# Layer 0's values into rows: three TensorE turnings of fp32, or one transposing DMA of two fp16 halves, in a two-layer graph transformer kernel on one core

## The chip, the core and the metric

The kernel runs on one core of one Trainium2 chip. The metric is the device time of one execution in microseconds, the median of several runs. The core has five engines that each follow an instruction stream of their own: TensorE (PE; its weight loads are shown apart as PEld), VectorE (DVE), ScalarE (ACT), GpSimd (POOL) and SyncE (SP), which here issues all the DMAs. The streams meet only at semaphores.

## What is computed

128 graphs of 128 nodes with 384 features go through two pre-norm attention layers of 12 heads (32 wide). The first masks its scores by the adjacency, the second takes the adjacency as a bias and has an output projection:

```python
h = relu(layernorm(x))                      # layer 0
q, k, v = h@Wq+bq, h@Wk+bk, h@Wv+bv         # 12 heads of 32
s = q@k.T/sqrt(32) + beta*adj;  s = where(adj > 0, s, -9e15)
x = x + softmax(s)@v                        # heads side by side
h = relu(layernorm(x))                      # layer 1
q, k, v = h@Wq.T, h@Wk.T, h@Wv.T+bv
x = x + (softmax(q@k.T*384**-0.5 + adj)@v)@Wo.T + bo
```

Everything is fp32 in and out. Where TensorE multiplies in fp16, a value is carried as two fp16 halves, high and low = value - high.

## The kernel before

**Units and phases.** Four graphs make a group and a group in one layer is a unit (`Unit`), 64 units in all. After the first few, units of layer 0 and layer 1 take turns. The kernel is a software pipeline over phases (`Phase`): in one phase one unit is normalised, the next older one is projected to q, k and v, the next is attended to, and the tail of the one before is finished. `run_phases` runs the first seven phases, then a loop of 12 pairs of phases a round, then the last ones. A phase has 12 slots (`SLOTS`), one for each chunk of four heads of a graph, so three slots a graph.

**The order is written out by hand.** Each engine's stream walks the slots and, within a slot, a few numbered places. A constant such as `O_T_AT = (3, 0)` says how many slots after the last chunk of a graph an operation stands, and at which place; `finished` turns that into slot and graph. Graph b's last chunk is slot 3b+2, so a constant (3, 0) puts the work of graphs 0, 1, 2 in slots 5, 8, 11 and that of graph 3 in slot 2 of the next phase, its tail. `NORM_SLOTS` does the same for the four norms of a phase (`normed_in`). `PROJ` spreads the 90 projection matmuls of a unit (ten jobs of nine, `project`, L999) over the slots: three counts a slot, for TensorE's places 0, 2 and 3. `HIGH_AT` and `LOW_AT` say where ScalarE and VectorE take a finished job's high and low half. No engine picks work; each takes its next instruction and waits if its semaphore is not there.

**Attention, per chunk.** TensorE makes scores (`scores`, L1012) two slots ahead, VectorE adds the bias and takes the maximum (`biased_scores`, L787) one slot ahead, ScalarE takes four exponentials with their sums (L667), TensorE turns the four fp32 probability tiles (`turn_probs`, L1022), and ScalarE copies them out of PSUM (`copy_turned`, L692). In layer 1 GpSimd also sums scores (L599, L605). After a graph's third chunk TensorE multiplies the turned probabilities with the values (`weigh_values`, L1035, into `o_bank`). The result lies feature by node, so it is the transpose of what the residual needs.

**Layer 0's way back to rows**, the part in question, once for each of 128 graphs:

- VectorE copies the 128x384 values of `o_bank` to `o_t` in SBUF, fp32 (`take_o`, L886), at (3, 0).
- TensorE turns the three 128x128 fp32 tiles of `o_t` into `post_bank` (`turn_rows`, L1050), at (3, 4).
- VectorE multiplies `post_bank` with the inverse softmax sums `inv0` into `o_rows` (`make_rows`, L908), at (4, 0).
- GpSimd adds the residual: `x_mid = x_res + o_rows` (`add_rows`, L618), at (4, 1). The layer-1 norm of the same group reads `x_mid`, in slots 0, 2, 3 and 5 of the phase in which graph 3's tail runs.

Layer 1 uses the same `post_bank` for its output projection (`project_out`, L1068 to L1072), after `norm_o` (L893), `high_o` on ScalarE (L706) and the low half on GpSimd (L644).

**The norm's own transposing DMA.** `split` (GpSimd, L585 to L590) leaves a graph's normalised rows as two fp16 halves in `h_rows`, [128, 2, 384], and SP brings them into `h` with one `dma_start_transpose` of six 128x128 tiles (L518), four for a unit. The q and k halves go to stacked buffers by plain DMAs, three for each of six jobs (`stack`, L483 and L487). All of these and the loads and stores (L496, L501, L509, L529, L539) stand in SP's one stream in a fixed order, and a wait there holds up what is behind it.

## Time and profile before

| | |
|---|---|
| median of 3 runs | 2221.32 us (2221.24 to 2221.51) |
| the profiled execution | 2218.76 us |
| its span, first to last instruction | 2216.9 us |
| busy share of the span | PE 97%, ACT 92%, DVE 82%, POOL 68% |
| mean granted TensorE clock | 0.998 |
| DMA | 303.38 MB, the queue's packets 71.2% of 16 engines' span |

Busy time is the union of an engine's instructions; issuing, waiting and branching do not count. A matmul's duration in the profile contains its way through the array, which the next matmul overlaps: what a matmul takes from the engine is the distance to the next one's start. Waits are inferred from semaphores. The profile is of one execution, 2.56 us under the median of the runs, and it leaves 1.9 us of its own time outside the span.

### The profile page before, as it was taken

To read this page: it belongs to the slowest core of one execution; us is meant where nothing else is said; L and a number is where in the kernel's file an instruction comes from. 1 tells how busy PE (TensorE), PEld (TensorE's weight loads), DVE (VectorE), ACT (ScalarE), POOL (GpSimd) and SP (SyncE) were. 2 spreads that over 40 slices of the span, in tenths; PEclk is the share of its full clock that TensorE was granted. 3 is DMA by queue.
4 is the path that set the end of the run, shared out by engine and by line. 5 is a ranking of instruction groups with operands and counts; after the bars stand their busy time and mean duration, and the time that the engine had idled before them with its cause. 6 is when DMAs were issued, how large, how long until landed. Compare 5 with 4: busy or idle time off the path is not lost.

```text
span 2216.9 us, 75650 instructions
## 1 busy us (share of the span) xinstructions
PE 2158.5 (97%) x19968; PEld 1422.1 (64%) x19968; DVE 1821.3 (82%) x10202; ACT 2049.2 (92%) x7824; POOL 1511.6 (68%) x2407
## 2 busy tenths in 40 slices
PE   5999999999999999999999999999999999999997
PEld 2566666666666666666666666666666666666665
DVE  5888888888888888888888888888888888888787
ACT  4999999999999999999999999999999999999987
POOL 1567766767667767667676677676676766776665
PEclk9999999999999999999999999999999999999999
DMA  9886776678678778675795686787767866766752
GB/s 191 168 134 140 130 138 147 130 131 157 126 137 138 137 143 141 132 143 125 134 159 127 136 139 136 145 136 137 143 130 135 154 130 134 146 132 134 133 103 60
DMA packets 461362, 303.38 MB, mean 137 GB/s; under 512 B 228481, under 2 KB 460929, under 8 KB 460929
## 3 DMA queue, kind: packets, MB, share of 16 engines
q1 hardware_dynamic: 460928, 298.45, 71.2%
q8 instruction: 169, 2.77, 0.6%
q14 instruction: 265, 2.16, 0.4%
HBM read 71.83 MB, written 25.17 MB: 44 GB/s over the span
## 4 chain that ended last, share of the span: by engine, by line
PE 84%; DVE 7%; ACT 4%; issue 3%; DMA 1%; SPq 0%; DVEq 0%; POOL 0%; ACTq 0%
PE job_bank L999 46%; PE pt_bank L1022 13%; PE o_bank L1035 8%; PE score_bank L1012 7%; ACT probs L667 3%; PE inv_bank L1058 3%; PE post_bank L1068 2%; PE post_bank L1069 2%; PE post_bank L1072 2%; PE post_bank L1050 2%; DVE neg L787 2%; DVE part_lo L865 1%; DVE inv_wide L857 1%; DMA x_norm<-in_x 1%; DVE off_zero L848 1%
## 5 line engine op out<-in xcount | busy, mean ns | idle before, releaser
L667 ACT ACTIVATE probs<-neg,neg_max 128x128 f32<-128x128 f32 x3072 | 1189.8, 394 | 47.0 <-DVE neg_max L787 47.0
L999 PE MATMUL job_bank<-h,w_hi 128*128 128x512 f16 x2304 | 725.9, 381 | 27.1 <-DMA h<-o_norm 21.6
L667 ACT ACTIVATION_READ_ACCUMULATOR probs<-neg,neg_max 128x1 f32 x3072 | 596.0, 194 | 0.0
L692 ACT ACTIVATE probs_t<-pt_bank 128x512 f32<-128x512 f32 x768 | 450.1, 586 | 32.0 <-PE pt_bank L1022 29.2
L1022 PE MATMUL pt_bank<-ident,probs 128*128 128x128 f32 x3072 | 464.2, 274 | 11.8 <-ACT probs_t L692 11.4
L999 PE MATMUL job_bank<-h,w_lo 128*128 128x512 f16 x1152 | 438.4, 381 | 0.0
L1022 PEld LDWEIGHTS pt_bank<-ident,probs 128*128 128x128 f32 x3072 | 365.9, 141 | 95.9 <-issue 14.0
L599 POOL TENSOR_TENSOR pair_sum<-neg 128x256 f32<-128x256 f32 x384 | 281.0, 732 | 196.0 <-DVE neg_max L787 180.8
L999 PE MATMUL job_bank<-w_hi,h 128*128 128x384 f16 x1536 | 413.9, 326 | 0.6 <-DVE v L879 0.3
L787 DVE CUSTOM_DVE_ANT_0 neg<-score_bank,bias 128x128 f32<-128x128 f32 x1536 | 354.1, 286 | 23.7 <-issue 22.2
L787 DVE CUSTOM_DVE_ANT_0 neg<-score_bank,adj 128x128 f32<-128x128 f32 x1536 | 353.8, 286 | 13.2 <-issue 10.5
L999 PEld LDWEIGHTS job_bank<-h,w_hi 128*128 128x128 f16 x2304 | 222.0, 98 | 217.4 <-issue 35.8
L1012 PEld LDWEIGHTS score_bank<-stack 96*128 96x128 f16 x3072 | 232.4, 97 | 126.5 <-DVE neg_max L787 6.3
L1012 PE MATMUL score_bank<-stack 96*128 96x128 f16 x3072 | 299.2, 219 | 5.3 <-DMA stack<-part_lo 5.3
L787 DVE DVE_READ_ACCUMULATOR2_ANT neg_max<- 128x1 f32 x3072 | 254.3, 83 | 0.6
L999 PE MATMUL job_bank<-w_lo,h 128*128 128x384 f16 x768 | 250.5, 326 | 0.0
L568 POOL TENSOR_TENSOR rstd<-shift_var,minus_half 128x1 f32<-128x1 f32 x256 | 144.8, 566 | 146.9 <-DVE shift_var L825 145.4
L590 POOL TENSOR_TENSOR h_rows<-h_rows 128x384 f16<-128x384 f32 x248 | 226.7, 914 | 20.7
L618 POOL TENSOR_TENSOR x_mid<-x_res,o_rows 128x384 f32<-128x384 f32 x128 | 127.9, 999 | 140.8 <-DVE o_rows L908 97.1
L1035 PE MATMUL o_bank<-probs_t,v 128*32 128x128 f32 x6144 | 220.8, 277 | 0.0
L870 DVE SCALAR_TENSOR_TENSOR part_lo<-job_bank,part_hi 128x512 f16<-128x512 f32 x192 | 132.5, 690 | 105.4 <-ACT part_hi L683 103.4
L605 POOL TENSOR_TENSOR four_sum<-pair_sum 128x128 f32<-128x128 f32 x384 | 176.6, 460 | 32.1
(75 smaller groups left out, 3507.6 us busy)
## 6 DMA issues: line engine op xcount, KB each, us to landing
stack<-part_hi SPq DMA_DIRECT2D x768, 128.0 KB, 3.5
stack<-part_lo SPq DMA_DIRECT2D x384, 128.0 KB, 3.8
x_res<-in_x SPq DMA_DIRECT2D x32, 768.0 KB, 5.8
out_x<-result_rows SPq DMA_DIRECT2D x128, 192.0 KB, 3.4
x_norm<-in_x SPq DMA_DIRECT2D x30, 768.0 KB, 6.2
adj<-in_adj SPq DMA_DIRECT2D x64, 256.0 KB, 3.8
h<-h_rows SPq DMA_TRANSPOSE x252, 3.9
x_norm<-in_x SPq DMA_DIRECT2D x4, 192.0 KB, 4.0
```

The lines of the kernel that those rows point to most:

```text
L568: pool.tensor_tensor(rstd[:, b:b + 1], shift_var[:, b, 1:2], minus_half[:, :], ALU.pow).then_inc(rstd_done, 1)
L590: pool.tensor_tensor(h_rows[b % 2][:, 1, :], h_rows32[:, :], h_rows[b % 2][:, 0, :], ALU.subtract).then_inc(h_rows_ready, 1)
L599: pool.tensor_tensor(pair_sum[:, :, :], neg[c % 2][:, :, 0:NODES // 2], neg[c % 2][:, :, NODES // 2:NODES], ALU.add).then_inc(pair_sum_don ...
L605: pool.tensor_tensor(four_sum[b % 2][:, first:first + HC, :], pair_sum[:, :, 0:NODES // 4], pair_sum[:, :, NODES // 4:NODES // 2], ALU.add ...
L667: last = act.activation(probs[c % 2][:, h, :], neg[c % 2][:, h, :], ACT.Exp, bias=neg_max[:, b, first + h:first + h + 1], scale=-1.0, accu ...
L692: act.activation(probs_t[b % 2][:, first:first + HC, :].rearrange("p h q -> p (h q)"), pt_bank[:, :], ACT.Copy).then_inc(probs_t_ready, 1)
L787: last = dve.tensor_tensor_reduce(out=neg[c % 2][:, h, :], in0=score_bank[c % 2][:, P * h:P * (h + 1)], in1=bias, scale=(-1.0 / SCORE0 if ...
L870: last = dve.scalar_tensor_tensor(part_lo[t][:, c, :], job_bank[j % 2][:, :], scale, part_hi[t][:, c, :], ALU.mult, ALU.subtract)
L999: last = pe.matmul(to, stationary, moving, start=(m == 0), stop=(m == MATMULS - 1))
L1012: last = pe.matmul(score_bank[c % 2][:, P * h:P * (h + 1)], q[0:3 * HEAD, c % KC, h, nodes], k[0:3 * HEAD, c % KC, h, nodes], start=True, ...
L1022: last = pe.transpose(pt_bank[:, P * h:P * (h + 1)], probs[c % 2][:, h, :], ident[:, :])
L1035: last = pe.matmul(o_bank[d:d + HEAD, f:f + P], v32[u.parity][:, b, HEAD * h:HEAD * (h + 1)], probs_t[b % 2][:, h, :], start=True, stop=True)
```

## The change

`take_o` no longer writes `o_t` in fp32. VectorE takes the high half of the values out of PSUM (`tensor_copy` to fp16), waits for it, and takes the low half with a second instruction (value minus high), both into `o_halves` [128, 2, 3, 128]. SP issues one `dma_start_transpose` of the six tiles of `o_halves` into `o_turned` (`turn_o`), after a wait on `o_taken`. GpSimd adds the two turned halves into `o_rows` (`add_halves`), VectorE multiplies `o_rows` in place with `inv0` (`make_rows`), and GpSimd adds the residual as before. TensorE's `turn_rows` is gone, and with it the sharing of `post_bank` between the layers (`free_post_bank`): `project_out` waits only for layer 1's own `result_ready`.

The places are laid out anew. The taking stays at (3, 0), the DMA's issue is at (3, 1), the adding of halves at (5, 0), the rows at (5, 1) (before: (4, 0)), the residual at (6, 0) (before: (4, 1)). Norms start in slots 0, 2, 4, 6 (before: 0, 2, 3, 5), the centring at (2, 0) and the norm's DMA at (3, 0); layer 1's high half of the output at (3, 3), its result at (6, 2) and its store at (7, 0) (before: (9, 0)). Both rows of `PROJ` spread the same 90 matmuls differently, and `HIGH_AT` and `LOW_AT` move for the jobs that end at TensorE's last place. The two norms of the first units that borrowed `o_t` and `o_norm` as buffers now borrow `o_halves` and `o_turned`.

```diff
 PROJ = (
-    ((1, 0, 1), (1, 0, 2), (3, 3, 2), (4, 0, 2), (0, 0, 4), (8, 0, 0), (7, 2, 5), (0, 0, 0),
-     (7, 7, 0), (4, 1, 0), (8, 3, 2), (0, 1, 12)),
-    ((0, 6, 0), (2, 6, 0), (0, 7, 1), (7, 0, 5), (0, 4, 0), (9, 1, 6), (2, 2, 0), (1, 0, 2),
-     (2, 7, 4), (0, 0, 2), (4, 0, 0), (7, 0, 3)),
+    ((4, 0, 0), (0, 0, 1), (1, 6, 3), (2, 0, 1), (1, 0, 4), (4, 1, 1), (5, 5, 3), (2, 3, 5),
+     (2, 5, 0), (4, 0, 0), (8, 2, 4), (0, 2, 11)),
+    ((1, 2, 2), (0, 9, 0), (0, 7, 0), (10, 0, 1), (1, 3, 3), (9, 2, 5), (0, 2, 2), (1, 3, 0),
+     (1, 7, 5), (1, 0, 2), (6, 0, 0), (3, 0, 2)),
 )
...
-HIGH_AT = ((0, 1), (0, 1), (1, 0))
-LOW_AT = ((0, 2), (0, 2), (1, 2))
+HIGH_AT = ((0, 1), (0, 1), (0, 3))
+LOW_AT = ((0, 2), (0, 2), (1, 1))
 MATMULS = 3 * KC
...
-NORM_SLOTS = (0, 2, 3, 5)
+NORM_SLOTS = (0, 2, 4, 6)
...
 MOMENTS_AT = (1, 1)
-CENTRE_AT = (1, 2)
+CENTRE_AT = (2, 0)
 SPLIT_AT = (2, 0)
-TURN_H_AT = (3, 1)
+TURN_H_AT = (3, 0)
 SCORES_AT = 4
...
 O_NORM_AT = (3, 2)
-O_HI_AT = (4, 0)
+O_HI_AT = (3, 3)
 O_LO_AT = (3, 1)
-TURN_ROWS_AT = (3, 4)
-O_ROWS_AT = (4, 0)
-X_MID_AT = (4, 1)
+TURN_O_AT = (3, 1)
+ADD_HALVES_AT = (5, 0)
+O_ROWS_AT = (5, 1)
+X_MID_AT = (6, 0)
 OUT_AT = (5, 1)
-RESULT_AT = (6, 0)
-STORE_AT = (9, 0)
+RESULT_AT = (6, 2)
+STORE_AT = (7, 0)
 KEEP_SLOTS = (3, 5, 7, 9)
...
         inv_t = sb("inv_t", [P, KC, P])
-        o_t = sb("o_t", [P, KC, P])
+
+        o_halves = sb("o_halves", [P, 2, KC, P], F16)
+        o_turned = sb("o_turned", [P, 2, KC, P], F16)
         o_norm = sb("o_norm", [P, KC, P])
...
                 return h_rows[b % 2]
-            return (o_t, o_norm)[b % 2][:, :, :].rearrange("p c q -> p (c q)").bitcast(F16).rearrange(
-                "p (l d) -> p l d", l=2)
+            if b == 2:
+                return o_halves[:, :, :, :].rearrange("p l c q -> p l (c q)")
+            return o_turned[:, :, :, :].rearrange("p l c q -> p l (c q)")
...
+            def turn_o(u, b):
+                n = u.group * GROUP + (b + 1)
+
+                if some(n - 1):
+                    sp.wait_ge(o_added, n - 1)
+
+                sp.sem_inc(o_turning, 1)
+                sp.wait_ge(o_taken, n)
+                sp.sem_inc(o_turning, 1)
+                sp.dma_start_transpose(o_turned[:, :, :, :].rearrange("p l c q -> p (l c) q"),
+                                       o_halves[:, :, :, :].rearrange("p l c q -> p (l c q)")).then_inc(o_turned_in, 16)
+
             def phase(p):
...
                     for place in range(2):
+                        u, b = finished(p, s, place, TURN_O_AT)
+                        if of_layer(u, b, 0):
+                            turn_o(u, b)
                         u, b = finished(p, s, place, STORE_AT)
...
+            def add_halves(u, b):
+                n = u.group * GROUP + (b + 1)
+                pool.wait_ge(o_turned_in, n * 16)
+                if some(n - 1):
+                    pool.wait_ge(x_mid_ready, n - 1)
+                pool.tensor_tensor(o_rows[:, :, :].rearrange("p h d -> p (h d)"),
+                                   o_turned[:, 0, :, :].rearrange("p c q -> p (c q)"),
+                                   o_turned[:, 1, :, :].rearrange("p c q -> p (c q)"), ALU.add).then_inc(o_added, 1)
+
             def add_rows(u, b):
...
                     for place in range(3):
+                        u, b = finished(p, s, place, ADD_HALVES_AT)
+                        if of_layer(u, b, 0):
+                            add_halves(u, b)
                         u, b = finished(p, s, place, X_MID_AT)
...
             def take_o(u, b):
+                n = u.group * GROUP + (b + 1)
                 dve.wait_ge(pv_done, u.n * GROUP + (b + 1))
-                if some(u.group * GROUP + b):
-                    dve.wait_ge(o_turned, u.group * GROUP + b)
-                dve.tensor_copy(o_t[:, :, :].rearrange("p c q -> p (c q)"), o_bank[:, 0:DIM]).then_inc(o_taken, 1)
+                if some(n - 1):
+                    dve.wait_ge(o_turned_in, (n - 1) * 16)
+                values = o_bank[:, 0:DIM]
+                high = o_halves[:, 0, :, :].rearrange("p c q -> p (c q)")
+                dve.tensor_copy(high, values).then_inc(o_high_taken, 1)
+                dve.wait_ge(o_high_taken, n)
+                dve.scalar_tensor_tensor(o_halves[:, 1, :, :].rearrange("p c q -> p (c q)"), values, 1.0, high,
+                                         ALU.mult, ALU.subtract).then_inc(o_taken, 1)
...
             def make_rows(u, b):
-                dve.wait_ge(o_turned, u.group * GROUP + (b + 1))
-                if some(u.group * GROUP + b):
-                    dve.wait_ge(x_mid_ready, u.group * GROUP + b)
-                dve.tensor_tensor(o_rows[:, :, :], post_bank[:, 0:DIM].rearrange("p (h d) -> p h d", h=HEADS),
+                dve.wait_ge(o_added, u.group * GROUP + (b + 1))
+                dve.tensor_tensor(o_rows[:, :, :], o_rows[:, :, :],
                                   inv0[:, b % 2, :].unsqueeze(2).to_broadcast([P, HEADS, HEAD]),
...
-            def free_post_bank(u, b):
-
-                if b > 0:
-                    pe.wait_ge(result_ready if u.layer == 1 else o_rows_ready, u.group * GROUP + b)
-                elif u.last is not None:
-                    pe.wait_ge(result_ready if u.last[0] == 1 else o_rows_ready, u.last[1] * GROUP + GROUP)
-
-            def turn_rows(u, b):
-                pe.wait_ge(o_taken, u.group * GROUP + (b + 1))
-                free_post_bank(u, b)
-                for c in range(KC):
-                    last = pe.transpose(post_bank[:, P * c:P * (c + 1)], o_t[:, c, :], ident[:, :])
-                last.then_inc(o_turned, 1)
-
             def turn_inverse(u, b):
...
                 n = u.group * GROUP + (b + 1)
-                free_post_bank(u, b)
+                if some(n - 1):
+                    pe.wait_ge(result_ready, n - 1)
                 pe.wait_ge(o_hi_ready, n)
...
                             scores(u, c)
-                        u, b = finished(p, s, place, TURN_ROWS_AT)
-                        if of_layer(u, b, 0):
-                            turn_rows(u, b)
                         u, b = finished(p, s, place, WEIGH_AT)
```

## Rows read from the trace of the kernel before

**Rows 1.** The page, part 1: busy us (share), instructions; part 4: the chain that ended last.

```profile
PE 2158.5 (97%) x19968; PEld 1422.1 (64%) x19968; DVE 1821.3 (82%) x10202; ACT 2049.2 (92%) x7824; POOL 1511.6 (68%) x2407
...
PE 84%; DVE 7%; ACT 4%; issue 3%; DMA 1%; SPq 0%; DVEq 0%; POOL 0%; ACTq 0%
```

**Rows 2.** Windows: 26 pairs of phases, then one layer-0 and one layer-1 phase.

```profile
core 0: us, PE busy (x) PEld busy (x) DVE busy (x) ACT busy (x) POOL busy (x), PEclk, DMA share, GB/s
...
251.60:2009.00 1757.40, 1745.88 (x16226) 1154.56 (x16224) 1466.42 (x8269) 1653.74 (x6345) 1237.13 (x1977) 1.00 0.73 138
...
1099.80:1131.90 32.10, 32.10 (x303) 21.19 (x302) 25.79 (x155) 30.52 (x122) 18.56 (x28) 1.00 0.80 121
1131.90:1167.10 35.20, 34.93 (x324) 23.16 (x323) 30.48 (x165) 32.98 (x124) 28.94 (x48) 1.00 0.74 155
```

**Rows 3.** Timeline of PE around one turning: start us, us, what.

```profile
1002.46 0.39 PE L1012 MATMUL score_bank<-stack 96*128 96x128 f16 x4
1002.69 0.50 PE L1050 MATMUL post_bank<-ident,o_t 128*128 128x128 f32 x3
1003.02 0.38 PE L999 MATMUL job_bank<-h,w_hi 128*128 128x512 f16 x1
```

**Rows 4.** Line L1050: duration ns min/median/max, first and last start us.

```profile
L1050 PE MATMUL post_bank<-ident,o_t x384: 272/273/281, 63.3 to 2116.6; 128*128 128x128 f32 x192
```

**Rows 5.** Groups by line and form: count | busy us, mean ns | idle before us.

```profile
L590 POOL TENSOR_TENSOR h_rows<-h_rows 128x384 f16<-128x384 f32 x248 | 226.7, 914 | 20.7
...
L870 DVE SCALAR_TENSOR_TENSOR part_lo<-job_bank,part_hi 128x512 f16<-128x512 f32 x192 | 132.5, 690 | 105.4 <-ACT part_hi L683 103.4
...
L618 POOL TENSOR_TENSOR x_mid<-x_res,o_rows 128x384 f32<-128x384 f32 x128 | 127.9, 999 | 140.8 <-DVE o_rows L908 97.1 <-issue 39.7 <-DMA x_res<-in_x 2.4
...
L857 DVE TENSOR_TENSOR inv_wide<-live,inv 128x384 f32<-128x384 f32 x128 | 79.8, 623 | 13.3
...
L908 DVE TENSOR_TENSOR o_rows<-post_bank,inv 128x384 f32<-128x384 f32 x128 | 71.0, 555 | 1.8
L886 DVE COPY o_t<-o_bank 128x384 f32<-128x384 f32 x128 | 71.0, 555 | 52.0 <-PE o_bank L1035 51.4
...
L835 DVE SCALAR_TENSOR_TENSOR h_rows<-centred,rstd,h_rows 128x384 f16<-128x384 f32 x4 | 2.5, 616 | 0.0
```

**Rows 6.** Line L518, the transposing DMA: issue ns; then us from issue to landing.

```profile
L518 SPq DMA_TRANSPOSE h<-h_rows x252: 1210/1242/2796, 8.9 to 2133.7; - x126
...
DMA to landing us min/median/max: 2.7/3.9/7.9
```

**Rows 7.** Timeline of SP in a layer-1 phase: start us, us, DMAs issued.

```profile
1138.08 0.60 SPq L487 DMA_DIRECT2D stack<-part_lo  x1
1140.24 1.19 SPq L483 DMA_DIRECT2D stack<-part_hi  x2
1141.48 0.60 SPq L487 DMA_DIRECT2D stack<-part_lo  x1
1142.38 1.26 SPq L518 DMA_TRANSPOSE h<-h_rows  x1
1143.77 1.21 SPq L483 DMA_DIRECT2D stack<-part_hi  x2
```

**Rows 8.** Timeline of DVE over the same graph: the taking, scores, the rows.

```profile
1137.92 0.56 DVE L886 COPY o_t<-o_bank 128x384 f32<-128x384 f32 x1 [0.34 <-PE o_bank L1035]
1138.40 0.28 DVE L787 CUSTOM_DVE_ANT_0 neg<-score_bank,adj 128x128 f32<-128x128 f32 x1
...
1139.25 0.55 DVE L813 BATCH_NORM_STATS2 stats<-x_mid 128x6 f32<-128x384 f32 x1
...
1140.95 0.56 DVE L908 TENSOR_TENSOR o_rows<-post_bank,inv 128x384 f32<-128x384 f32 x1
```

**Rows 9.** Waits in the whole span: us in total, times, longest.

```profile
PE job_bank L999 <- DMA h<-o_norm: 21.6, 1, 21.6
```

**Rows 10.** Waits in the same 26 pairs: us in total, times, longest.

```profile
ACT probs L667 <- DVE neg_max L787: 36.9, 53, 1.0
```

More of the change, by code:

```diff
@@ L135, in __init__ @@
     def __init__(self, attend=None, project=None, norm=None, tail=None, look=None, bias=None, keep=None,
-                 weights=None, table=None, begin=0, norm_slots=NORM_SLOTS):
+                 weights=None, table=None, begin=0, norm_slots=None):
         self.attend, self.project, self.norm, self.tail = attend, project, norm, tail
         self.look, self.bias, self.keep, self.weights = look, bias, keep, weights
-        self.table, self.begin, self.norm_slots = table, begin, norm_slots
+        self.table, self.begin, self.norm_slots = table, begin, norm_slots or NORM_SLOTS
     def counts(self):
@@ L417, in build @@
         pv_done = sem("pv_done")
+        o_high_taken = sem("o_high_taken")
         o_taken = sem("o_taken")
@@ L422, in build @@
         inv_t_ready = sem("inv_t_ready")
-        o_turned = sem("o_turned")
+        o_turning = sem("o_turning")
+        o_turned_in = sem("o_turned_in")
+        o_added = sem("o_added")
         o_rows_ready = sem("o_rows_ready")
```

## The prediction

> **What bounds the kernel now.** The page comes first: TensorE is busy 97% of the span, ScalarE 92%, VectorE 82%, GpSimd 68%, and the chain that ended last runs over TensorE for 84% of it [rows 1]. A share of the whole span hides the stages, so the windows come next. Over 26 pairs of phases, 1757.4 us or 67.6 us a pair, TensorE is idle 11.5 us, ScalarE 103.7, VectorE 291.0 and GpSimd 520.3; in one layer-0 phase TensorE is busy 32.10 of 32.10 us, and in the layer-1 phase after it 34.93 of 35.20, at full granted clock [rows 2]. Busy could still mean waiting inside a matmul's modelled end. The timeline rules that out where it matters: the three turnings start right behind the scores, and 0.33 us after their start the next projection starts (1002.69 to 1003.02) [rows 3]. TensorE issues without a pause and sets the pace; ScalarE is a near second, with 4.0 us free a pair (103.7/26), and is nearest in the layer-0 phase: 30.52 busy of 32.10.
>
> **The change, part by part.** Durations are of the profiled execution, 2218.76 us, 1.9 us over its span and 2.56 under the median of the runs.
>
> *Removed from TensorE:* 128 turnings of three tiles at 0.33 us [rows 3] = 42.2 us. A single one is shown as 273 ns long [rows 4], but what it takes from the engine is 0.11. All of it lies on the engine that sets the end: minus 42.2 us, or 1.3 us a pair. `turn_rows`' wait on `o_taken` and the wait for `post_bank` go too; no row shows either ending an idle time, so nothing is booked for them.
>
> The Trainium skill (TensorE: Matmul & The Clock Gate, Part 4: PE-mode transpose) gives about 275 ns for a transpose inside a kernel. The row has the same duration, 273, but a pitch of 0.11; by the page's figure the sum would have 384 x 0.275 = 106 us in place of 42.
>
> *Added to VectorE:* the copy is there already (555 ns, L886, the same size from PSUM [rows 5]); to fp16 I leave it unchanged. The second taking is a subtraction to fp16: the same form on 384 columns out of SBUF takes 616 ns (L835), on 512 columns out of PSUM 690 (L870) [rows 5]. I take 0.6, plus about 0.1 for the wait between the two: 0.7 x 128 = 90 us. `make_rows` reads SBUF where it read PSUM; L857, which reads only SBUF, has a mean of 623 against 555 [rows 5], so 0 to 9 us more. Of a pair's 11.2 us of idle VectorE (291.0/26) these take 2.8, and the shorter pair another 1.3: about 7.1 us are left, 1.8 us a graph. That is the cover; without it the 2.8 us would be on the path and the kernel 48 us slower (2.8 less 1.3, times 32).
>
> *Added to GpSimd:* one addition of two fp16 tensors to fp32. L590 takes 914 ns to fp16, L618 999 in fp32 [rows 5]; 0.91 x 128 = 117 us, into 520 us of idle time in the middle alone [rows 2]. Hidden, unless it comes late, which is the next term.
>
> *Added to SP and the DMA engines:* 128 transposing DMAs of the shape that L518 has 252 times: 1.24 us of issue, landing 3.9 us after it in the median, 2.7 to 7.9 [rows 6]. SP is not short of time: between issues it waits 0.2 to 1.6 us [rows 7]. But the new one waits in SP's order for `o_taken`, and behind it stand the slot's stack DMAs, loads and stores. `take_o` stands at place 0 of the same slot, so that wait is about the 1.2 us of the two takings; the stacks are read a phase later. The engines carry 0.73 of their time now [rows 2], and this adds half as many transposing transfers again. Bounds for the price: zero if the landing stays at 3.9, up to 4 us a graph if it goes to the 7.9 that was once seen.
>
> *The way round.* Before, the copy starts at 1137.92 and the rows at 1140.95, 3.0 us, with one round of scores between [rows 8]. Now it is 1.2 (two takings) + 3.9 (landing) + 0.9 (adding) = 6.0 us before `make_rows` may start. The places give two slots of 2.8 us (67.6/24), and the four scores of the slot ahead of it, 0.85 us (1138.40 to 1139.25 [rows 8]): 6.5. It fits by 0.5 us in the median and not in the slow landings. When it does not, GpSimd and VectorE both stand, and behind VectorE stand the next scores and then ScalarE.
>
> *Moved:* the last norm goes from slot 5 to 6, because `x_mid` of graph 3 now comes in slot 5. Its DMA is issued in slot 9 instead of 8; TensorE needs it three slots, 8.4 us, later, against 3.9 of landing. Only the start shows a wait of that kind, 21.6 us, once [rows 9], and its norm slots stay. Result, store, high half and low half move by places within a slot or forward by two: nothing. `PROJ` puts the same 90 matmuls elsewhere, at a cost between the 11.5 us of idle time that it could remove and as much again that it could bring; I take zero, since TensorE hardly pauses now [rows 2].
>
> *Given back.* ScalarE waits 36.9 us in the middle for VectorE's scores [rows 10]. VectorE's idle time falls from 11.2 to 7.1 us a pair, 1.6 times less; if these waits grow as much, by 22 us, and a third of that reaches TensorE, it is 8 us. Ends: 0 if none does, 22 if all does.
>
> Sum: 2218.8 - 42.2 + 8 = 2184.6 for a profiled execution; with the 2.56 us by which the median of the runs lies above it, **2187 us**.
>
> **The rivals.**
>
> *ScalarE or VectorE takes much of it (0.20).* For it: in the layer-0 phase ScalarE has 1.58 us free of 32.10 [rows 2] and TensorE would give up three turnings there, 1.0 us; two engines at 97% each rarely interlock without loss. Against: 0.6 us stay even then, and 2.2 in the layer-1 phase. Half the gain goes: 2221 - 21 = 2200, from 2195 to 2214.
>
> *Nothing is left (0.07).* The same, with the whole 42 us given back: 2217 to 2226, about 2220.
>
> *The round trip is late (0.11).* The mechanism is the one wait of GpSimd for the landing in slot s+2 (L618's neighbour, `add_halves`), with VectorE's rows and the next scores behind it. The landing has 6.5 - 1.2 - 0.9 = 4.4 us; what is above that comes first out of the 1.8 us a graph that VectorE still has, then out of the gain (0.33 a graph). So it decides from a mean landing of 6.5 us on. At 6.9, three over the median, 0.7 us a graph is left, 90 us, less 42: 2269 us. For it: 7.9 has been seen [rows 6], and the new DMAs join engines at 0.73. Against: the median of 252 is 3.9.
>
> The Trainium skill (VectorE: DVE Perf Modes, The three transpose paths, and its Rules for kernel authors) says to turn 128x128 on TensorE where PSUM will do as destination, and gives the DMA 1309 ns for one in 2-byte elements. By it six tiles one after another would be 7.9 us and the change a loss, by the rival's arithmetic. The trace disagrees: six tiles land in 3.9, issue included.
>
> *The turnings cost their shown duration (0.01).* If each took 273 ns of TensorE [rows 4], 384 of them would be 104.8 us and the time 2114. The start of the next projection 0.33 us after three of them speaks against it. (The Trainium skill's figure for a transpose, in the section cited above, would have it so.)
>
> **How the numbers follow.** My forecast, most of the 42 us kept, has 0.61; within it 2168 (nothing given back, and TensorE's last 11.5 us of idle time reduced by the new plan) to 2195. With the second case the kernel is faster in 0.82. I count within 0.2% as no change, about 4.4 us, which is what a measurement of this kernel can tell; that is 0.07. Slower is the late round trip, 0.11. The range takes my case, the second and the near part of the third: 2168 to 2219.
>
> **What would show it.** In the profile after: no L1050; TensorE still idle under 1% in the middle window and the pair near 66.5 us. VectorE busy about 1.5 us more a pair net. The new DMA's median landing under 4.4 us, and waits of GpSimd's halves on it short and few. ScalarE's waits for VectorE's scores at most 60 us in the middle. I am wrong if TensorE's idle time rises to 2 us a pair or more: if then its releaser is ScalarE's exponentials, the second case holds; if GpSimd's wait for the landing comes ahead of VectorE's, the late round trip. A pair that shortens by more than 1.9 us would mean that the plan alone was worth something, which no row here shows.

## The result and the profile after

The kernel after takes 2388.74 us (2384.65 to 2390.36, 4 runs) against 2221.28 for the kernel before beside it (2217.97 to 2221.51, 4 runs): a ratio of 1.0754, 95% interval 1.0739 to 1.0769. It is 167 us slower, where 34 us faster was forecast, and it lies outside the range.

The profile's page of the kernel after, parts 1, 3 and 4 (busy time; queue; the chain), and 5 and 6 for the new path:

```profile
PE 2188.1 (92%) x19584; PEld 1367.6 (57%) x19584; DVE 1956.9 (82%) x10330; ACT 2045.8 (86%) x7824; POOL 1649.4 (69%) x2535
...
q1 hardware_dynamic: 563328, 323.63, 78.2%
...
ACT 22%; PE 22%; issue 17%; DVE 16%; POOL 7%; SPq 6%; DMA 5%; DVEq 1%; ACTq 0%; POOLq 0%
...
L946 DVE TENSOR_TENSOR o_rows<-o_rows,inv 128x384 f32<-128x384 f32 x128 | 115.5, 902 | 151.0 <-POOL o_rows L635 150.7
L635 POOL TENSOR_TENSOR o_rows<-o_turned 128x384 f32<-128x384 f16 x128 | 116.7, 912 | 169.9 <-DMA o_turned<-o_halves 169.7
...
o_turned<-o_halves SPq DMA_TRANSPOSE x128, 3.8
```

Windows of the kernel after: the same 26 pairs, then one layer-0 and one layer-1 phase:

```profile
core 0: us, PE busy (x) PEld busy (x) DVE busy (x) ACT busy (x) POOL busy (x), PEclk, DMA share, GB/s
279.40:2170.50 1891.10, 1769.42 (x15912) 1107.42 (x15912) 1579.26 (x8373) 1649.89 (x6344) 1349.31 (x2080) 1.00 0.80 139
1196.20:1232.50 36.30, 32.53 (x299) 20.14 (x297) 27.89 (x157) 30.19 (x121) 20.44 (x30) 1.00 0.97 132
1232.50:1269.60 37.10, 35.35 (x315) 22.33 (x316) 32.94 (x167) 33.24 (x125) 31.20 (x50) 1.00 0.82 143
```

Against [rows 1, 2]: the chain no longer runs over TensorE (84% then, 22% now) but over everything in turn, DMA and SP among it. TensorE's idle time in the middle rose from 11.5 to 121.7 us (1891.1 - 1769.4), ScalarE's from 103.7 to 241.2. The pair went from 67.6 to 72.7 us, 133.7 of the 171.4 us by which the spans differ; 27.8 came before the window, 9.9 behind it. ScalarE's busy time did not move (1653.7 and 1649.9): it stands and waits.

Waits of the kernel after, whole span (us in total, times, longest):

```profile
POOL o_rows L635 <- DMA o_turned<-o_halves: 169.7, 66, 6.6
DVE o_rows L946 <- POOL o_rows L635: 150.7, 82, 5.0
...
ACT probs L701 <- DVE neg_max L821: 137.5, 35, 6.5
...
PEld job_bank L1037 <- DVE v L913: 92.2, 52, 3.3
PE job_bank L1037 <- DVE v L913: 89.0, 58, 3.7
```

Read from the top it is one cascade: GpSimd waits for the landing, VectorE for GpSimd, and ScalarE and TensorE for what VectorE has standing behind its wait. The chain of waits shows it for graph 1 of the layer-0 phase above:

```profile
1219.32 0.56 SPq L490
1219.92 0.60 SPq L490
1220.57 0.60 SPq L494
...
1221.44 5.91 DMA o_turned<-o_halves
1227.35 0.07 issue
1227.41 0.92 POOL o_rows L635
1228.36 0.06 DVE o_rows L946
```

And the timelines of VectorE and ScalarE in the same stretch (start, us, what, idle time before it in brackets):

```profile
1219.95 0.55 DVE L923 CAST o_halves<-o_bank 128x384 f16<-128x384 f32 x1
1220.54 0.56 DVE L925 SCALAR_TENSOR_TENSOR o_halves<-o_bank,o_halves 128x384 f16<-128x384 f32 x1
...
1228.36 0.56 DVE L946 TENSOR_TENSOR o_rows<-o_rows,inv 128x384 f32<-128x384 f32 x1 [3.15 <-POOL o_rows L635]
1228.83 0.55 DVE L913 SCALAR_TENSOR_TENSOR v<-job_bank,bv_rows 128x384 f32<-128x384 f32 x1
...
1232.53 0.40 ACT L701 ACTIVATE probs<-neg,neg_max 128x128 f32<-128x128 f32 x1 [3.91 <-DVE neg_max L821]
```

From the first taking to the rows it is 8.4 us where 6.0 were booked; here most of the excess is the landing, 5.91 us. VectorE stands 3.15 of them, with a `v`, a taking, a bias and the next scores behind, and ScalarE then stands 3.91.

### The profile page after: what moved, and what is told of

It is laid out like the page before. It is cut to its first block, busy times and chain, and to the rows that moved or that the text cites. A ratio compares the mean times of both kernels' runs of the same rounds, so it can differ in the third digit from the quotient of the medians.

```text
span 2388.3 us, 75448 instructions
## 1 busy us (share of the span) xinstructions
PE 2188.1 (92%) x19584; PEld 1367.6 (57%) x19584; DVE 1956.9 (82%) x10330; ACT 2045.8 (86%) x7824; POOL 1649.4 (69%) x2535
## 4 chain that ended last, share of the span: by engine, by line
ACT 22%; PE 22%; issue 17%; DVE 16%; POOL 7%; SPq 6%; DMA 5%; DVEq 1%; ACTq 0%; POOLq 0%
ACT probs L701 14%; PE job_bank L1037 8%; DMA o_turned<-o_halves 5%; PE pt_bank L1060 4%; DVE neg L821 3%; ACT probs_t L726 3%; POOL o_rows L635 3%; SPq L490 2%; PE o_bank L1073 2%; DVE part_lo L899 2%; PE inv_bank L1082 2%; ACT centred L751 2%; ACT part_hi L717 2%; PE score_bank L1050 2%; POOL pair_sum L621 1%
## 5 line engine op out<-in xcount | busy, mean ns | idle before, releaser
L1037 PE MATMUL job_bank<-h,w_hi 128*128 128x512 f16 x2304 | 724.3, 382 | 74.2 <-DVE v L913 50.1
L1060 PE MATMUL pt_bank<-ident,probs 128*128 128x128 f32 x3072 | 474.2, 277 | 51.8 <-ACT probs_t L726 41.4
L726 ACT ACTIVATE probs_t<-pt_bank 128x512 f32<-128x512 f32 x768 | 450.0, 586 | 35.7 <-PE pt_bank L1060 35.5
L1060 PEld LDWEIGHTS pt_bank<-ident,probs 128*128 128x128 f32 x3072 | 351.7, 141 | 196.6 <-issue 106.0
L1037 PE MATMUL job_bank<-w_hi,h 128*128 128x384 f16 x1536 | 410.0, 329 | 52.6 <-DVE v L913 38.9
L1037 PE MATMUL job_bank<-h,w_lo 128*128 128x512 f16 x1152 | 439.8, 382 | 0.0
L621 POOL TENSOR_TENSOR pair_sum<-neg 128x256 f32<-128x256 f32 x384 | 294.1, 766 | 108.1 <-DVE neg_max L821 88.7
L1037 PEld LDWEIGHTS job_bank<-h,w_hi 128*128 128x128 f16 x2304 | 216.7, 98 | 245.4 <-issue 49.1
L1050 PE MATMUL score_bank<-stack 96*128 96x128 f16 x3072 | 301.2, 220 | 5.0 <-DMA stack<-part_lo 5.0
L1050 PEld LDWEIGHTS score_bank<-stack 96*128 96x128 f16 x3072 | 237.1, 98 | 117.3 <-issue 8.5
L1037 PE MATMUL job_bank<-w_lo,h 128*128 128x384 f16 x768 | 252.8, 329 | 0.0
L612 POOL TENSOR_TENSOR h_rows<-h_rows 128x384 f16<-128x384 f32 x248 | 232.0, 936 | 20.7
L946 DVE TENSOR_TENSOR o_rows<-o_rows,inv 128x384 f32<-128x384 f32 x128 | 115.5, 902 | 151.0 <-POOL o_rows L635 150.7
L635 POOL TENSOR_TENSOR o_rows<-o_turned 128x384 f32<-128x384 f16 x128 | 116.7, 912 | 169.9 <-DMA o_turned<-o_halves 169.7
L1037 PEld LDWEIGHTS job_bank<-w_hi,h 128*128 128x128 f16 x1536 | 149.7, 98 | 139.6 <-DVE v L913 49.3
```

Source lines behind the costliest of these rows:

```text
L612: pool.tensor_tensor(h_rows[b % 2][:, 1, :], h_rows32[:, :], h_rows[b % 2][:, 0, :], ALU.subtract).then_inc(h_rows_ready, 1)
L621: pool.tensor_tensor(pair_sum[:, :, :], neg[c % 2][:, :, 0:NODES // 2], neg[c % 2][:, :, NODES // 2:NODES], ALU.add).then_inc(pair_sum_don ...
L635: pool.tensor_tensor(o_rows[:, :, :].rearrange("p h d -> p (h d)"), o_turned[:, 0, :, :].rearrange("p c q -> p (c q)"), o_turned[:, 1, :, ...
L726: act.activation(probs_t[b % 2][:, first:first + HC, :].rearrange("p h q -> p (h q)"), pt_bank[:, :], ACT.Copy).then_inc(probs_t_ready, 1)
L946: dve.tensor_tensor(o_rows[:, :, :], o_rows[:, :, :], inv0[:, b % 2, :].unsqueeze(2).to_broadcast([P, HEADS, HEAD]), ALU.mult).then_inc(o_ ...
L1037: last = pe.matmul(to, stationary, moving, start=(m == 0), stop=(m == MATMULS - 1))
```

## Experiments

Each time is that of one execution, except e15 (the median of ten). The kernel before took 2218.2 to 2221.5 us beside them, and the four executions of the kernel after lie 5.7 us apart, so differences of up to about 6 us distinguish nothing. "Pair" is the mean of the 26 pairs: 67.6 us before, 72.7 after.

### e1 to e4: the plan, the landing, the transfer, the rows

**e1**: after's plan (norm slots, `PROJ`, `HIGH_AT` and the rest), with TensorE's three turnings back at their old places.

```diff
-ADD_HALVES_AT = (5, 0)
-O_ROWS_AT = (5, 1)
-X_MID_AT = (6, 0)
+TURN_ROWS_AT = (3, 4)
+O_ROWS_AT = (4, 0)
+X_MID_AT = (4, 1)
```

> The new plan (PROJ, norm slots, centring, high and low halves, result and store places) with the old way back to rows: copy, three turnings on TensorE, rows at (4, 0), residual at (4, 1). Theory 1, the late round trip through the DMA (2388.3 - 2216.9 = 171 us more span, of which GpSimd waits 170 us for the landing and VectorE 151 us behind it): the plan by itself costs little, 2200 to 2260 us. Theory 2, the plan is what is bad (new counts of projection matmuls a slot, the store's wait in SP's queue, 245 us): 2340 us or more.

**e2**: after, but GpSimd adds the halves as they stand in `o_halves`; the DMA is issued and read by nobody, so layer 0's values stay unturned. Only the next taking and SP's next issue wait for its landing.

```diff
-                pool.wait_ge(o_turned_in, n * 16)
+                pool.wait_ge(o_taken, n)
...
-                                   o_turned[:, 0, :, :].rearrange("p c q -> p (c q)"),
-                                   o_turned[:, 1, :, :].rearrange("p c q -> p (c q)"), ALU.add).then_inc(o_added, 1)
+                                   o_halves[:, 0, :, :].rearrange("p c q -> p (c q)"),
+                                   o_halves[:, 1, :, :].rearrange("p c q -> p (c q)"), ALU.add).then_inc(o_added, 1)
```

> The changed kernel with all its instructions and its DMAs, but GpSimd adds the halves straight from o_halves after the taking (the rows are then left unturned), and only the next taking waits for the landing. Theory 1, late round trip: 2180 to 2230 us, since TensorE is rid of the turnings and nobody waits. Theory 3, it is not the latency but the work that was added (second taking, rows out of SBUF at 902 ns against 555, the DMAs' traffic and SP's time): 2330 us or more.

**e3**: e2 with the DMA left out as well (values unturned).

```diff
-                        if of_layer(u, b, 0):
+                        if False:
                             turn_o(u, b)
```

> As the run before it, and the transposing DMA is left out altogether (rows left unturned). Theory 1: the same as the run before it within 10 us. Theory 4, the traffic and SP's issue time hurt: 20 us or more under the run before it.

**e4**: after, with the inverse sums multiplied in by GpSimd, right behind its addition.

```diff
+            def scale_rows(u, b):
+                n = u.group * GROUP + (b + 1)
+                pool.wait_ge(inv0_ready, n)
+                pool.wait_ge(o_added, n)
+                pool.tensor_tensor(o_rows[:, :, :], o_rows[:, :, :],
```

> The changed kernel, full computation, with the multiplication by inv0 moved from VectorE to GpSimd right behind the adding of halves, so that VectorE never waits for the round trip and does not run it beside a GpSimd addition. Theory 1 in its form 'the cost is VectorE standing behind the landing, with scores and values queued there': 2190 to 2260 us. If instead GpSimd's own wait (scores' sums queued behind it in layer 1) or TensorE's plan is what costs: 2340 us or more.

| | us | pair | layer-1 phase | layer-0 phase |
|---|---|---|---|---|
| before | 2221.3 | 67.6 | 35.4 | 32.2 |
| after | 2388.7 | 72.7 | 37.0 | 35.7 |
| e1 | 2312.8 | 70.7 | 37.4 | 33.3 |
| e2 | 2346.0 | 71.3 | 37.3 | 34.0 |
| e3 | 2285.1 | 69.3 | 37.4 | 31.8 |
| e4 | 2394.3 | 72.9 | 38.3 | 34.6 |

Within the new plan the transfer costs 103.6 us: 42.8 of it the wait of its reader (e2), 60.8 the rest (e3). The rest is partly still a wait, the next taking's, as the waits of e2 show:

```profile
DVE o_halves L924 <- DMA o_turned<-o_halves: 75.5, 31, 4.5
```

In e3 the layer-0 phase is under before's, yet the whole is 64 us slower than before: 37.4 us in the layer-1 phase has nothing to do with the transfer. And e1 is 91.5 us slower with no transfer at all, between the two ranges expected. Either the plan costs as much again, or it suits the new path. e4 takes the slowed `make_rows` (last section) from VectorE and gains nothing.

### e5: before's plan with after's path

```diff
-HIGH_AT = ((0, 1), (0, 1), (0, 3))
-LOW_AT = ((0, 2), (0, 2), (1, 1))
+HIGH_AT = ((0, 1), (0, 1), (1, 0))
+LOW_AT = ((0, 2), (0, 2), (1, 2))
...
-CENTRE_AT = (2, 0)
+CENTRE_AT = (1, 2)
...
-TURN_H_AT = (3, 0)
+TURN_H_AT = (3, 1)
...
-O_HI_AT = (3, 3)
+O_HI_AT = (4, 0)
```

(`PROJ`, `RESULT_AT` and `STORE_AT` go back too. The norm slots stay 0, 2, 4, 6.)

> The changed kernel with its DMA path and its places for it, and the plan of before for the rest: PROJ, high and low halves, centring, the norm's DMA, layer 1's high half, result and store (norm slots stay 0, 2, 4, 6). If the plan and the late round trip add up (the new plan alone measured 92 us over the kernel before): about 2388 - 92 = 2296 us, the layer-1 phase back at 35 to 36 us and the layer-0 phase still long in its last slot. If the new plan is bad only with the old path and is what the DMA path needs: 2380 us or more.

2384.6 us, pair 72.7 (36.4 in the layer-1 phase and 36.3 in the layer-0 phase). The kernel after is 4 us slower, within the spread. The new plan cost 92 us in e1 with TensorE's turnings, and e3 is 26 us over e11 (below), which has neither turnings nor transfer and the old plan. So the costs are not additive, and taking the new plan away does not make this change fast.

### e6 to e10: time for the landing

**e6** gives graphs 0 to 2 one more slot, doubles `o_halves`, and makes the rows in `x_mid`, so that the next taking no longer waits for the landing just before it. `o_turned` stays single. **e7** is e6 with before's plan; **e8** is e7 with the issue moved ahead of the slot's stacks; **e9** is e7 with layer 0's norms back at 0, 2, 3, 5; **e10** is e9 with layer 1's as well.

```diff
-ADD_HALVES_AT = (5, 0)
-O_ROWS_AT = (5, 1)
-X_MID_AT = (6, 0)
+ADD_HALVES_AT = ((6, 0),) * 3 + ((5, 0),)
+O_ROWS_AT = ((6, 1),) * 3 + ((5, 1),)
+X_MID_AT = ((7, 0),) * 3 + ((6, 0),)
...
-        o_halves = sb("o_halves", [P, 2, KC, P], F16)
+        o_halves = [sb(f"o_halves{b}", [P, 2, KC, P], F16) for b in range(2)]
```

e8, against e7, and e9 against e7:

```diff
-TURN_O_AT = (3, 1)
+TURN_O_AT = (2, 1)
```

```diff
-TURN_H_AT = (3, 1)
+TURN_H_AT = (3, 0)
...
+        self.norm_slots = norm_slots or (NORM_SLOTS if norm and norm.layer == 1 else (0, 2, 3, 5))
```

> The changed kernel with one slot more for the round trip of graphs 0, 1 and 2 (halves added at (6, 0), rows (6, 1), residual (7, 0)), two buffers for the taken halves so that the next taking does not wait for the landing, and the rows made in x_mid itself. Late round trip: VectorE's wait before the rows in the layer-0 phase falls from 4.1 us to under 1, and the time to that of the run without the transfer, 2280 to 2310 us. If traffic and SP's order cost by themselves: 2340 us or more.

> As the run before it, with the plan of the kernel before for the rest. If the two causes are separate and together all there is: 2180 to 2215 us, under the kernel before (2221), since TensorE has 42 us less to do. If TensorE's gain cannot be had at all: 2225 us or more.

> As the run before it, with the transfer one slot earlier in SP's order ((2, 1) for (3, 1)), ahead of the three stack DMAs that stood before it. SP's delay between the end of the taking and the issue (1.7 us for graph 1 in the changed kernel) goes to about 0.1. If that delay still matters: 5 to 20 us under the run before it. If the slot more covered it: within 5 us. If the stacks are the ones that must not wait: over it.

> The later round trip with the old plan (2322 us), and the norms of layer-0 units back in slots 0, 2, 3, 5 (they do not read x_mid), their transposing DMA at (3, 0). In the run before it TensorE began each projection of a layer-0 unit with a wait: the last graph's h landed 1.6 us after the phase began, 4.7 us of it between the rows being ready and the issue. If that is the third cause: the wait goes and the time is 2240 to 2275 us. If it is not what sets the phase: 2310 us or more.

> As the run before it, and layer 1's norms in slots 0, 2, 3, 5 too, as in the kernel before; the residual is then added one slot earlier, at place 2, right behind the rows. All of the old plan but the way back to rows itself. If the layer-1 phase is long (36 to 38 us against 35.3) because centring, deviation and statistics came to share a slot with other work: 10 to 40 us under the run before it, and if everything is right near 2200. If VectorE's longer work for the rows is what makes it long: within 10 us of the run before it.

| | us | pair | layer-1 phase | layer-0 phase |
|---|---|---|---|---|
| e6 | 2355.1 | 71.5 | 39.6 | 31.9 |
| e7 | 2322.4 | 70.6 | 38.0 | 32.6 |
| e8 | 2410.6 | 73.6 | 41.1 | 32.5 |
| e9 | 2346.2 | 71.6 | 39.2 | 32.4 |
| e10 | 2339.2 | 71.2 | 39.0 | 32.3 |

One slot more, with the second buffer, takes 62 us off (e5 to e7): the layer-0 phase falls from 36.3 to 32.6. That is where the late landing sat. But the layer-1 phase grows by 1.6, and the cure of SP's order is the worst run of all. Its waits say what became late instead:

```profile
ACT part_hi L716 <- PE job_bank L1043: 140.2, 58, 6.6
...
PE job_bank L1043 <- DMA h<-h_rows: 114.2, 32, 6.1
```

TensorE stands for `h`, because SP holds up the norm's transfer. SP's own waits in e8 say for what:

```profile
SPq L508 <- POOL x_mid L644: 222.0, 32, 9.2
SPq L510 <- DVE o_halves L930: 124.8, 63, 4.7
```

In e7 the same two are 33.1 and 17.7 us. The second is the wait for `o_taken`. The first and longer one is for GpSimd's addition of the graph before: `o_turned` has one buffer. For graphs 1 to 3 that addition stands in slot 3b+5, and e8 moves the issue into slot 3b+4, ahead of it. So e8 does not try SP's order alone, and with a second `o_turned` it might have come out otherwise; no run has one. In e9, moving that transfer ahead put it in front of the new one, and GpSimd's wait rose from 153.2 us in e7 to:

```profile
POOL x_mid L645 <- DMA o_turned<-o_halves: 207.8, 40, 9.0
```

In both runs, what was moved ahead in SP's one stream made something else late.

TensorE's clock takes part in these times too. After most of TensorE's waits of 2 to 6 us its granted clock is 1.2 GHz for a few us in place of 2.4. A window of the kernel after, behind a wait of 2.58 us for a `v` (the columns as above, granted clock 0.50):

```profile
789.00:795.80 6.80, 5.74 (x26) 3.71 (x24) 4.87 (x30) 3.78 (x17) 3.24 (x5) 0.50 0.24 63
```

A 128x512 matmul of L1037 takes 634 ns at that clock in the median, and 379 at the full one. Summed over the execution the lower clock lasts 7 us in the kernel before, 38 in the kernel after, 60 in e7, 82 in e5 and 151 in e8. Half of that is the most that it can cost. So part of what is put down to a wait is the slower work behind it: up to 19 us in the kernel after, and in e8 TensorE is busy 36 us longer than in e7 with the same instructions. It also blurs e5 against the kernel after, with up to 22 us in favour of the latter.

### e11, e13, e14, e16: before's plan without the transfer

**e11** is e5 without the DMA (GpSimd adds from `o_halves`, values unturned) and with layer 0's norms at 0, 2, 3, 5. **e13** puts layer 1's norms there too, `X_MID_AT` at (5, 2). **e14** is e11 with one taking, the high half added to itself. **e16** is e11 with the rows multiplied on GpSimd, as e4. e14 against e11:

```diff
-                dve.tensor_copy(high, values).then_inc(o_high_taken, 1)
-                dve.wait_ge(o_high_taken, n)
-                dve.scalar_tensor_tensor(o_halves[:, 1, :, :].rearrange("p c q -> p (c q)"), values, 1.0, high,
-                                         ALU.mult, ALU.subtract).then_inc(o_taken, 1)
+                dve.tensor_copy(high, values).then_inc(o_taken, 1)
```

> The changed kernel without its transposing DMA (the halves are added as they are taken, rows left unturned), with the old plan and layer 0's norms in their old slots. It is what the change would be if the transfer cost nothing. If the transfer's time, its place in SP's order and its traffic are all of the loss: 2185 to 2215 us, 5 to 35 us under the kernel before. If VectorE's and GpSimd's added work (second taking, halves, rows out of SBUF) eats TensorE's 42 us: 2221 us or more.

> The run without the transfer and with the old plan (2259 us), and layer 1's norms too back in slots 0, 2, 3, 5, with the residual added one slot earlier, right behind the rows (place 2 of the rows' slot). If the moved norm makes the layer-1 phase long (ScalarE waits 0.9 us a phase for its statistics there): 2215 to 2240 us. If VectorE's added work does: 2250 us or more.

> The same run (2259 us), without VectorE's second taking (the high half is added to itself; rows unturned and of half precision). If the 0.6 us more a graph on VectorE is the cause: 2215 to 2240 us. If it lies in idle time, as the prediction had it: 2250 us or more.

> The same run (2259 us), with the rows scaled on GpSimd, so that VectorE has no instruction with two SBUF operands beside a GpSimd addition (548 to 1348 ns for it in the changed kernel) and no wait for GpSimd. If that collision and wait are the cause: 2220 to 2245 us. If not: within 8 us of 2259, or over it because GpSimd's sums come late.

e11 2259.0, e13 2263.3, e14 2240.3, e16 2277.8 us. So the transfer, with the waits it brings and the lower clock behind them (82 us of it in e5, 12 in e11), costs 126 us (e5 less e11; layer 0's norms stand earlier in e11). Even for nothing it would leave the kernel 38 us slower than before, though the turnings are gone from all four. The second taking is 18.7 us of that. The windows of e11 and e14 over the 26 pairs:

```profile
258.40:2043.00 1784.60, 1734.83 (x15914) 1111.40 (x15913) 1555.97 (x8373) 1645.76 (x6345) 1347.75 (x2080) 1.00 0.71 136
```

```profile
256.30:2024.10 1767.80, 1730.94 (x15914) 1113.21 (x15912) 1504.97 (x8269) 1647.09 (x6345) 1339.38 (x2080) 1.00 0.69 137
```

VectorE is idle 228.6 us in e11, 13% of the stretch, and taking 51.0 us of work from it shortens the stretch by 16.8. An engine with idle time on average was on the path for a third of the added work.

### e12: before with an idle transfer

A transposing DMA per graph, from a constant to a spare buffer, at the new one's place in SP's stream and with its wait on `o_taken`. No engine waits for it.

```diff
+                sp.wait_ge(o_taken, n)
+                sp.sem_inc(o_turning, 1)
+                sp.dma_start_transpose(
+                    o_idle[:, :, :, :].rearrange("p l c q -> p (l c) q"),
+                    w_hi[0][:, 0:2, :].rearrange("p l d -> p (l d)")).then_inc(o_idle_in, 16)
```

> The kernel before, and with each layer-0 graph one transposing DMA of the same shape at the same place in SP's order (after the same wait on o_taken), from a constant into a spare buffer; no engine waits for it. It prices SP's issue time and order and the traffic alone. If they are harmless, as the prediction had it: within 5 us of the kernel before. If they hold up the norm's own transfer and the stacks (rows ready to issue 3.1 us before, 4.7 in the later runs): 20 to 80 us over it.

2247.1 us, 26 more than the kernel before beside it. TensorE's wait for the stacks, a single one of 5.3 us in the kernel before, is now:

```profile
PE score_bank L1031 <- DMA stack<-part_lo: 24.8, 23, 5.3
```

So 128 transfers that nobody reads already cost what all the turnings were worth (e17). This run does not part SP's order from the DMA engines' load. SP's wait for `o_taken` is 4.6 us in all there; it also waits 21.0 us for the landing of the idle transfer before.

### e15: only the graph with time to spare

Before, with graph 3 of each group, 32 of 128, by DMA, its rows at (5, 1) and residual at (5, 2); TensorE turns the others. Nothing is left out.

```diff
-O_ROWS_AT = (4, 0)
-X_MID_AT = (4, 1)
+O_ROWS_AT = ((4, 0),) * 3 + ((5, 1),)
+X_MID_AT = ((4, 1),) * 3 + ((5, 2),)
...
+                        if of_layer(u, b, 0) and b == GROUP - 1:
+                            turn_o(u, b)
```

> The kernel before, full computation, its plan untouched; only the last graph of each group goes back to rows by the transposing DMA (32 of 128), at the place where SP was free in every run (0.1 us from taking to issue, landing 2.8 us) and TensorE sets the pace (35.0 of 35.3 us). TensorE saves 32 x 0.33 = 10.6 us. If that is kept: 2210 to 2218 us, a version under both. If VectorE's 0.6 us more and the later rows cost as much in that phase: 2219 to 2240 us.

2219.96 against 2220.16 us, ratio 1.000 (0.9991 to 1.001): no difference. GpSimd waits 1.3 us in all for these landings, so none is late. The 10.6 us of turnings (32 x 0.33) saved are given back elsewhere. It is the best version with a transfer that computes everything, and it only equals the kernel before.

### e17 and e18: what the turnings are worth

**e17** is before with `turn_rows` left out: the rows come from `o_t`, unturned, at the old place. **e18** is e17 with the rows at (5, 1), the residual at (6, 0) and layer 1's norms at 0, 2, 4, 6.

```diff
-                        if of_layer(u, b, 0):
+                        if False:
                             turn_rows(u, b)
```

> The kernel before with the 384 turnings left out and nothing in their place: VectorE scales the rows out of o_t itself at the old place (rows unturned). It prices the one term of gain. The prediction's 42 us: 2179 us. If VectorE and ScalarE take over the pace at once: 2195 to 2215 us, the layer-0 phase still 31.5 us or more.

> As the run before it, with the rows at (5, 1), the residual at (6, 0) and layer 1's norms in slots 0, 2, 4, 6, as the way round by the DMA needs them. If the later places cost nothing, as the prediction had it: within 5 us of the run before it. If they make the layer-1 phase long (36.4 us in every run that has them): 20 to 40 us over it, in the layer-1 phase alone.

2195.2 and 2217.2 us. The windows over the 26 pairs of e17, one layer-0 phase of it, and the 26 pairs of e18:

```profile
248.30:1987.00 1738.70, 1718.17 (x15914) 1116.99 (x15912) 1488.18 (x8269) 1641.96 (x6345) 1252.71 (x1976) 1.00 0.75 140
```

```profile
1087.90:1119.50 31.60, 31.60 (x298) 20.54 (x297) 25.81 (x156) 30.41 (x122) 18.95 (x28) 1.00 0.72 119
```

```profile
254.90:2002.90 1748.00, 1721.59 (x15913) 1114.65 (x15912) 1482.28 (x8269) 1649.53 (x6344) 1260.27 (x1976) 1.00 0.74 139
```

Removing the turnings with nothing in their place gives 25.5 us, not 42.2, so that is about the most that this change could have won as the rest stands (its `make_rows` reads SBUF, with a median of 715 ns, so it keeps that part of the change's cost). The later rows, residual and norms alone (e18) take 22.0 back: 9.3 in the middle, and 12.7 at the start and the end. For TensorE's three turnings the rows were 3.0 us away [rows 8]; a way round that needs these later places pays this before it has moved a byte.

## Why the prediction was wrong

From one execution each, the whole adds up as follows. The order is one of several, and since e1 and e5 show that parts do not add up, each size holds in its place of the row only.

| step | from, to | us |
|---|---|---|
| turnings off TensorE | before, e17 | -25.5 |
| rows, residual and layer 1's norms later | e17, e18 | +22.0 |
| GpSimd's addition, and what it slows | e18, e14 | +23.1 |
| second taking | e14, e11 | +18.7 |
| the transfer: wait, SP, traffic, clock (layer 0's norms later too) | e11, e5 | +125.7 |
| the new plan (within the spread) | e5, after | +4.1 |

**What bounds the kernel: half right.** TensorE did set the pace, but only 25.5 of 42.2 us came free (e17). Per pair it is 0.7 us, not 1.3. The second case's "half the gain goes" was nearer to that than the 8 us that I gave back.

**"All of it lies on the engine that sets the end": 42.2 booked, 25.5 measured.** In the middle TensorE's busy time fell by 27.7 us (1745.9 to 1718.2) where 104 rounds of 0.33 would be 34.3; its idle time rose by 9.0 (11.5 to 20.5), and the stretch shortened by the difference, 18.7. So the pitch was somewhat too long a price, and a third of what did come free was given back. In the layer-0 phase ScalarE is then busy 30.41 of 31.60 us, but TensorE is still shown busy for all 31.60, so that ScalarE is what took the rest is likely and not shown.

**"About 7.1 us are left, 1.8 us a graph. That is the cover": wrong.** The length of the added instructions was right (L925 has a mean of 558 ns, 600 booked), but idle time averaged over a pair is not cover at the place. Leaving out one VectorE instruction a graph was worth 18.7 us, of the 71.3 us that it lasts in all (e11, e14).

**`make_rows` "0 to 9 us more": mis-sized.** It took 115.5 us of VectorE against 71.0 [rows 5]; e4 and e16 show that moving it to GpSimd does not help. Why it is longer stands in the last section.

**GpSimd's addition, hidden: partly.** Its length was right (912 ns, 914 booked). Yet e14, which lacks both the transfer and the second taking, is 23.1 us over e18, most of it in the layer-1 phase (36.4 against 35.6 us). VectorE's rows wait only 8.2 us for GpSimd in e14, but they are slower beside it, 101.8 us in all against 86.9. GpSimd's busy time rises by 79 us in the middle. How the rest divides stays open.

**"SP is not short of time": wrong.** Time between issues was taken for room in the order. In e12, 26 us slower, TensorE waits longer for the stacks, and in e8, 88 us over e7, for the norm's `h`; e12 leaves the DMA engines' load as a second cause, e8 the single `o_turned` and the clock. And the wait to issue was not "about the 1.2 us of the two takings" alone. In the 26 pairs of the kernel after, worked from the trace, it is 2.67 us more in the median for graph 0 and 1.65 for graph 1, where stacks and a norm's transfer stand ahead; for graphs 2 and 3 it is 0.09.

**The landing: right, and it did not help.** The new DMA lands 3.8 us after issue in the median (3.9 booked); the bound of 4.4 held, and a mean of 6.5 was never needed.

**"It fits by 0.5 us in the median": this is the step that failed.** Giving it one slot more, and a second buffer for the halves, won 62 of the 126 us back (e7). The way round, from the start of the taking to that of the rows, is 8.6 us in the median for graphs 0 and 1, where 6.0 were booked. Part of it is the wait to issue, and part the landing, 4.5 in the median for graph 1. And the two slots were taken at the mean of 2.8 us, while slots 8 and 9 of the layer-0 phase, just where graph 1 turns round, are 2.6 and 2.0 us long in the kernel before (by the starts of the exponentials, the mean of 25 phases), 4.6 in place of 5.6 together. VectorE stands 3.4 us a time in the mean before graph 1's rows, and 0.7 and less before the others'. The mechanism of the third case came, at its place and with the sign that it gave: GpSimd's wait, 169.7 us, ahead of VectorE's, 150.7. Its point of decision was wrong, so 0.11 was far too little. It was put at a mean landing of 6.5 us; the loss came at 3.9. Nothing was set down for the time ahead of the issue. Its 2269 us would have been short too: it priced the late rows alone.

**ScalarE's waits "at most 60 us in the middle": 110.0.** They come in 26 waits of up to 5.9 us, where before it was 36.9 us in 53 of up to 1.0.

**Moved places at nothing.** The rows, residual and norms cost 22.0 us (e18); the norm that went from slot 3 to 4 was not even listed. `PROJ` and the rest cost from nothing measurable to 92 us, depending on the path (e5, e1).

The Trainium skill (VectorE: DVE Perf Modes, Rules for kernel authors) prefers TensorE for a 128x128 transpose where PSUM will do, and gives 1309 ns for one by DMA (The three transpose paths). Its advice came true here, but not by that figure: six tiles land in 3.8 us, not 7.9, and most of the loss sits in the waits around them.

**Left open:** how the 126 us divide between waiting, SP's order, the lower clock and load on the DMA engines (their share is 0.97 in one layer-0 phase of the kernel after, 0.80 in one before), and why the new plan costs 92 us with TensorE's turnings and none that can be told apart with the transfer. A lead that no run follows: SP stands 242.0 us before layer 1's stores in e1, and 43.5 in the kernel before.

## What to carry to other kernels

A DMA round trip between two engines costs more than its landing: add the wait of the issuing queue behind what stands ahead of it, take the slots' own lengths at that place rather than their mean, and count who is queued behind the reader's wait. Before replacing work on the busiest engine, run the kernel with that work simply left out; if that gives 25 us, a replacement in the same plan will hardly give more. Then put in the replacement's transfer with nobody waiting for it; here these two runs, 25.5 us won and 25.6 lost, already cancel, which is a warning and not yet a sum.

## Hardware behaviour not expected

`make_rows` has one form and one size, and yet no one duration. It read PSUM before; now both inputs are in SBUF. Line L908 of e1 (inputs in PSUM and SBUF), then L946 of the kernel after (both in SBUF); duration ns min/median/max:

```profile
L908 DVE TENSOR_TENSOR o_rows<-post_bank,inv x128: 545/557/559, 64.8 to 2209.0; 128x384 f32<-128x384 f32 x128
```

```profile
L946 DVE TENSOR_TENSOR o_rows<-o_rows,inv x128: 548/804/1348, 70.4 to 2292.0; 128x384 f32<-128x384 f32 x128
```

Timeline of the kernel after, one of the long ones beside GpSimd:

```profile
1217.58 0.99 POOL L662 TENSOR_TENSOR x_mid_bo<-x_mid,bo_rows 128x384 f32<-128x384 f32 x1
...
1217.65 1.33 DVE L946 TENSOR_TENSOR o_rows<-o_rows,inv 128x384 f32<-128x384 f32 x1 [1.64 <-POOL o_rows L635]
```

It ends 0.41 us after GpSimd's addition does. That holds throughout: of the 128, 36 run with no GpSimd instruction beside them and take 554 to 560 ns; 90 start under one, and end 0.41 us after it in the median (0.40 to 0.42 for the middle eight tenths; one ends before it). With an input in PSUM none of 128 is over 559 ns, although 64 run beside GpSimd.

The Trainium skill (SBUF — State Buffer, Who interferes with whom) says that a VectorE instruction with two SBUF inputs contends with a GpSimd instruction that reads SBUF, over a shared port pair that is an exclusive lock, and that the order of issue decides who blocks. The trace agrees for VectorE as the later one, with the 0.41 us above. So reading the rows from SBUF rather than PSUM added 44.5 us of VectorE time (115.5 - 71.0).
